# A drain of GpSimd's queue in front of its waits for gather buffers and indices, in a two-layer graph network

## The chip, the cores and the metric

The kernel runs on one NeuronCore of one Trainium2 chip. The metric is the device time of one execution in microseconds. A profile is one more execution, recorded by the hardware profiler; its durations are those of that execution alone.

## The reference, cut to what matters

There are 8 batches of 2048 nodes with 256 features, and a 0/1 adjacency matrix for each batch. Layer 0 takes, for each node, its first 25 neighbours and the elementwise maximum of their normalised rows. Layer 1 is an attention layer over the same adjacency matrix.

```python
h = jnp.maximum(_layernorm(x, axis=-1), 0.0)          # layer 0
pri = -jnp.arange(N, dtype=jnp.float32)
vals, idx = jax.lax.top_k(jnp.where(adj != 0, pri, -jnp.inf), 25)
agg = where(vals > -inf, vmap(lambda x, i: x[i])(h, idx), -inf).max(axis=2)
agg = where(degree <= 25, maximum(agg, 0.0), agg)
x = x + relu(concatenate([h, agg], -1) @ W0 + b0)
h = jnp.maximum(_layernorm(x, axis=-1), 0.0)          # layer 1
g = h @ W1; s1, s2 = g @ a1, g @ a2
att = softmax(where(adj > 0, leaky_relu(s1[:, :, None] + s2[:, None, :], 0.4), -1e20), axis=1)
x = x + gelu(att @ g)
```

## The kernel before, in words

A tile is 128 nodes; a batch has 16 tiles and the kernel 128. Each engine has a program of its own, written out by hand, and the programs meet in semaphores only. A round is one batch: in round b the engines work at layer 0 of batch b and, with `old` and `new`, at layer 1 of batch b - 1. Round 0 has layer 0 alone, and a last round without layer 0 (`drain=True` in the code, which has nothing to do with the instruction of that name) finishes layer 1 of batch 7.

**Layer 0 of a tile.** ScalarE turns a tile's adjacency rows into 0/1 (`sign`, L384), TensorE transposes them into PSUM `ps_c` (`transpose_signs`, L875), ScalarE copies them out (`evacuate_signs`, L388 and L390), TensorE packs them into words (`make_words`, L883 to L887), and VectorE searches the words for the first 25 neighbours (`search`, L596 to L647), which ends with the tile's list of indices `idx` and the semaphore `idx_ready`. `idx` has two buffers. GpSimd then gathers, for each of the 25 neighbours, 128 rows of 1 KB from the table of normalised rows `h_table` in HBM, one row for each partition: 25 indirect DMAs of 128 rows, all from L372. They fill two buffers: `gb0` takes the first 13 neighbours and `gb1` the other 12 (`CHUNKS = (13, 12)`). Each buffer exists once.

VectorE reduces a buffer by the maximum (`chunk_max`, L657). The reduction of `gb0` writes into a free slot of `gb1`, and the reduction of `gb1` writes `hl`. Each reduction ends with an increment of `maxed[0]` or `maxed[1]`, which tells GpSimd that the buffer is free. In VectorE's program, step v has the reduction of `gb1` of tile v first, then the search and the statistics, then the reduction of `gb0` of tile v + 1, and layer 1's work on both sides of it. A gather tells of its landing in the semaphores `gathered[0]` and `gathered[1]`, for which VectorE waits before a reduction.

**GpSimd's program** is nothing but these gathers. For each tile it waits for `idx_ready`, then for `maxed[0]`, issues 13 gathers, waits for `maxed[1]`, and issues 12. The helper `wait_apart` makes each wait an instruction of its own, followed by an increment of `pool_passed`, so that the wait stands in the sequencer and not in a gather. The sequencer may be some gathers ahead of the engine's processors, which write the descriptors. At the start of each batch there are two more waits, for the stores of `h_table` (`hn_stored`); the change leaves them alone.

**Layer 1 of a tile** takes two items (128 columns of attention each). For an item: ScalarE L437 turns edges into a bias, VectorE L717 (first half of a round, all 2048 columns) or L713 (second half, 1024 columns) adds it, ScalarE L444, VectorE L735, ScalarE L451 or L454 (exponential), VectorE L745, TensorE L895 into `ps_av`.

Of the kernel before, what the change touches and what calls it, by code (L numbers as in the profile page):

```python
# [68 lines left out]
def graph_layers(nc, x, adj, W0, b0, W1, a1, const_f, const_i, out):  # L69
    ctx = ExitStack()  # L70
    with ctx:
# [124 lines left out]
        def wait_apart(engine, name, semaphore, value):  # L196

            engine.wait_ge(semaphore, value)
            engine.sem_inc(S[name], 1)
# [155 lines left out]
        @block.gpsimd  # L355
        def _(pool):
            nc.gpsimd.memset(zeros[:, :], 0.0).then_inc(S["zeros_ready"], 1)
            pool.wait_ge(S["zrow_stored"], 32)
            with pool.Fori(0, NB, 2) as b2:
                for tb in range(2):  # L360
                    b = b2 + tb
                    for u in range(2):
                        wait_apart(pool, "pool_passed", hn_stored[u], b * 64 + 64)
                    with pool.Fori(0, PAIRS) as i:
                        for u in range(2):
                            g = b * TILES + i * 2 + u
                            wait_apart(pool, "pool_passed", S["idx_ready"], g + 1)
                            k = 0
                            for c, n in enumerate(CHUNKS):
                                wait_apart(pool, "pool_passed", maxed[c], g + 1)  # L370
                                for s in range(n):
                                    pool.indirect_dma_start(gb[c][:, s + (c > 0), :], None, table[tb],  # L372
                                                            bass.IndirectOffsetOnAxis(idx[u][:, k:k + 1], 0)
                                                            ).then_inc(gathered[c], 16)
                                    k += 1
# [635 lines left out]
```

## Time and profile before

| | |
|---|---|
| time, median of 3 runs | 4714.1 us (4710.35 to 4717.25) |
| span of the profiled execution | 5921.6 us |
| VectorE busy in it | 3609.4 us, 61% |
| GpSimd busy in it | 3420.3 us, 58% |
| TensorE busy in it | 2583.7 us, 44% |
| ScalarE busy in it | 2320.3 us, 39% |
| DMA queues, share of 16 engines | 23.8% (gathers), 18.1% (all other transfers) |
| gathers | 3200, 419.64 MB |

The profiled execution has no time of its own beside its span of 5921.6 us, from the first to the last instruction of the program; what lies around it isn't told. It is 1207.5 us longer than the median of the runs. Busy time counts instructions of the engines; the sequencers' waits and branches aren't counted.

### The profile page before, as it was taken

What the parts mean: (1) busy time and instruction counts of PE and PEld (TensorE: products, weight loads), DVE (VectorE), ACT (ScalarE), POOL (GpSimd) and SP (SyncE); (2) the same over time, 40 slices, a digit from 0 to 9 for tenths busy, and PEclk for the clock granted to TensorE, in tenths of its full rate; (3) what the DMA queues carried; (4) which work ended last, traced back from release to release, by engine and by line L of the source; (5) the groups of instructions that cost most, each with busy time, mean ns of one, the idle gap of its engine ahead of it and who ended that gap; (6) DMA issues with size and microseconds to landing.
All of it is one profiled execution on the core that took longest, in us unless ns stands there. A gap on an engine that the chain in (4) does not pass through costs nothing.

```text
span 5921.6 us, 48215 instructions
## 1 busy us (share of the span) xinstructions
PE 2583.7 (44%) x13568; PEld 1939.9 (33%) x13568; DVE 3609.4 (61%) x6299; ACT 2320.3 (39%) x2505; POOL 3420.3 (58%) x3205
## 2 busy tenths in 40 slices
PE   1332334444445334434455344444445435444357
PEld 1221223333333233323333233333334323333236
DVE  4454557566666566555677555666567656666567
ACT  2121234333444335333354333544335333434248
POOL 3655565555666566664677546466567665665530
PEclk9555556566666676666667666666666667666679
DMA  4434434344444444444444444344444444443322
GB/s 148 131 114 135 133 120 132 111 132 144 144 128 125 132 152 127 129 125 140 149 143 153 134 130 142 111 135 152 143 124 152 134 136 148 138 129 122 118 75 71
DMA packets 397876, 775.86 MB, mean 131 GB/s; under 512 B 64739, under 2 KB 245862, under 8 KB 381286
## 3 DMA queue, kind: packets, MB, share of 16 engines
q0 software_dynamic: 153600, 419.64, 23.8%
q1 hardware_dynamic: 244070, 353.77, 18.1%
q8 instruction: 93, 1.52, 0.1%
q14 instruction: 113, 0.93, 0.0%
HBM read 689.26 MB, written 83.89 MB: 131 GB/s over the span
## 4 chain that ended last, share of the span: by engine, by line
another core or an unknown queue 34%; issue 17%; ACT 14%; PE 12%; DVE 9%; POOL 1%; DMA 0%; ACTq 0%; DVEq 0%; SPq 0%; POOLq 0%
PE ps_av L895 4%; PE ps_l L923 3%; ACT stage L390 2%; ACT lk L444 2%; ACT lk L451 2%; ACT nbt L437 2%; PE ps_l L941 1%; ACT sg L384 1%; DVE hl L657 1%; DVE val L717 1%; PE ps_l L924 1%; POOL gb L372 1%; PE ps_l L943 1%; ACT y L498 1%
## 5 line engine op out<-in xcount | busy, mean ns | idle before, releaser
L372 POOL DMA_INDIRECT gb<-h_table,idx x3200 | 3419.6, 1069 | 2275.2 <-DVE gb L657 1039.9
L895 PE MATMUL ps_av<-hz,lk 128*128 128x256 f32 x3840 | 1136.2, 456 | 158.1 <-issue 85.7
L895 PEld LDWEIGHTS ps_av<-hz,lk 128*128 128x128 f32 x3840 | 878.6, 235 | 403.5 <-issue 252.5
L934 PE MATMUL ps_t<-cf,y 128*128 128x128 f32 x256 | 84.3, 430 | 2055.4 <-ACT y L498 1615.6
L388 ACT ACTIVATE sg<-ps_c 128x2048 bf16<-128x2048 bf16 x128 | 240.2, 1877 | 1813.7 <-remote 1673.1
L735 DVE SCALAR_TENSOR_TENSOR lk<-val,lk 128x2048 f32<-128x2048 f32 (+1 forms) x240 | 421.2, 1755 | 674.9 <-ACT lk L444 613.2
L657 DVE TENSOR_REDUCE hl<-gb 128x256 f32<-128x3328 f32 x128 | 746.8, 5834 | 83.6 <-DMA gb<-h_table,idx 67.2
L657 DVE TENSOR_REDUCE gb<-gb 128x256 f32<-128x3328 f32 x128 | 741.0, 5789 | 30.9 <-DMA gb<-h_table,idx 26.0
L934 PEld LDWEIGHTS ps_t<-cf,y 128*128 128x128 f32 x256 | 36.0, 197 | 2080.2 <-ACT y L498 1634.1
L923 PE MATMUL ps_l<-w,hcat 128*128 128x256 f32 x1024 | 407.2, 567 | 600.6 <-ACT hcat L485 505.2
L923 PEld LDWEIGHTS ps_l<-w,hcat 128*128 128x128 f32 x1024 | 277.5, 284 | 693.1 <-ACT hcat L485 483.4
L444 ACT ACTIVATE lk<-val,s2p 128x2048 f32<-128x2048 f32 (+1 forms) x240 | 379.4, 1581 | 271.5 <-remote 165.7
L717 DVE CUSTOM_DVE_ANT_0 val<-nbt,s_all 128x2048 f32<-128x2048 bf16 x120 | 274.0, 2283 | 292.0 <-ACT nbt L437 158.1
L437 ACT ACTIVATE nbt<-edge 128x2048 bf16<-128x2048 uint8 (+1 forms) x240 | 356.7, 1486 | 59.4 <-DVE m_t L717 39.8
L522 ACT COPY h_acc<-ps_l 128x257 f32<-128x257 f32 (+1 forms) x128 | 47.8, 373 | 825.2 <-remote 554.2
L941 PE MATMUL ps_l<-w,h1t 128*128 128x257 f32 x512 | 270.1, 666 | 71.7 <-issue 55.1
L804 DVE SCALAR_TENSOR_TENSOR x<-ps_l,xl 128x256 f32<-128x256 f32 x128 | 54.1, 422 | 325.4 <-PE ps_l L924 213.2
L384 ACT ACTIVATE sg<-ad 128x2048 bf16<-128x2048 int32 x128 | 243.3, 1901 | 6.1 <-DMA ad<-in_adj 6.1
L451 ACT ACTIVATE lk<-lk,nb 128x2048 f32<-128x2048 f32 x120 | 240.2, 2001 | 13.1 <-DVE lk L735 13.1
L390 ACT ACTIVATE stage<-ps_c 128x2048 uint8<-128x2048 bf16 (+1 forms) x128 | 239.6, 1872 | 0.0
L918 PE MATMUL ps_t<-cf,hl 128*128 128x128 f32 x512 | 102.3, 324 | 275.6 <-DVE hl L657 197.4
L713 DVE TENSOR_TENSOR val<-nbt,s_all 128x1024 f32<-128x1024 bf16 x120 | 146.0, 1216 | 108.5 <-ACT nbt L437 91.3
(95 smaller groups left out, 3767.9 us busy)
## 6 DMA issues: line engine op xcount, KB each, us to landing
ad<-in_adj SPq DMA_DIRECT2D x128, 1024.0 KB
edge<-edges_t SPq DMA_DIRECT2D x128, 512.0 KB
gb<-h_table,idx POOLq DMA_INDIRECT x3200
edges_t<-stage SPq DMA_DIRECT2D x32, 1024.0 KB
xl<-in_x SPq DMA_DIRECT2D x128, 128.0 KB
hl<-h_table SPq DMA_DIRECT2D x128, 128.0 KB
x_rows<-x SPq DMA_DIRECT2D x128, 128.0 KB
xo<-x_rows SPq DMA_DIRECT2D x16, 1024.0 KB
```

Of the source, the lines that this page charges most:

```text
L372: pool.indirect_dma_start(gb[c][:, s + (c > 0), :], None, table[tb], bass.IndirectOffsetOnAxis(idx[u][:, k:k + 1], 0)).then_inc(gathered[c ...
L384: nc.scalar.activation(sg[:, :], ad[u][:, :], ACT.Sign).then_inc(S["signed"], 1)
L390: nc.scalar.activation(stage[:, :, bass.ds(col, P)], sgt.rearrange("p (m n) -> p m n", n=P), ACT.Relu).then_inc(S["edges_ready"], 1)
L437: nc.scalar.activation(blocked_of(jj, drain)[:, cols], edge[u][:, jj, cols], ACT.Identity, scale=BLOCKED, bias=-BLOCKED).then_inc(S["block ...
L444: nc.scalar.activation(lk_of(jj, u, drain)[:, 0:w], val[jj][:, 0:w], ACT.Relu, scale=1 - SLOPE, bias=s2p[:, bass.ds(j, 1)]).then_inc(S["re ...
L451: nc.scalar.activation(q[:, :], q[:, :], ACT.Exp, bias=bias, accum_out=za[:, bass.ds(j, 1)]).then_inc(S["exp_ready"], 1)
L657: V.tensor_reduce(dst, gb[c][:, :, :].rearrange("p k c -> p c k"), AX.X, ALU.max).then_inc(maxed[c], 1)
L717: V.tensor_tensor_reduce(out=val[jj][:, :], in0=off[:, :], in1=s1_all[:, :], scale=1.0, scalar=-3e38, op0=ALU.add, op1=ALU.max, accum_out= ...
L735: V.scalar_tensor_tensor(out=q[:, 0:w], in0=val[jj][:, 0:w], scalar=SLOPE, in1=q[:, 0:w], op0=ALU.mult, op1=ALU.add).then_inc(S["leaky_rea ...
L895: ins = T.matmul(ps_av[:, k * C:(k + 1) * C], lk_of(jj, u, drain)[:, k * P:(k + 1) * P], hz[jj][:, :], start=False, stop=False)
L923: T.matmul(ps_l[:, 0:C], hcat[:, k, :], w0[:, k, :], start=k == 0, stop=False)
L941: T.matmul(ps_l[:, 0:C + 1], h1t[:, k, :], w1[:, k, :], start=k == 0, stop=k == 1)
```

## The change

GpSimd's sequencer gets a drain instruction in front of the wait for `maxed[0]` and in front of the wait for `maxed[1]`: two in each tile, 256 in all. A drain holds the sequencer until what it has handed to the engine is done. The wait for the indices moves behind the first of the two. All waits, their values, the gathers and their order stay as they are.

```diff
                         for u in range(2):
                             g = b * TILES + i * 2 + u
-                            wait_apart(pool, "pool_passed", S["idx_ready"], g + 1)
                             k = 0
                             for c, n in enumerate(CHUNKS):
+                                pool.drain()
+                                if c == 0:
+                                    wait_apart(pool, "pool_passed", S["idx_ready"], g + 1)
                                 wait_apart(pool, "pool_passed", maxed[c], g + 1)
                                 for s in range(n):
                                     pool.indirect_dma_start(gb[c][:, s + (c > 0), :], None, table[tb],
```

## Rows read from the trace of the kernel before

**Rows 1.** The page: span, busy time by engine, chain that ended last.

```profile
span 5921.6 us, 48215 instructions
...
PE 2583.7 (44%) x13568; PEld 1939.9 (33%) x13568; DVE 3609.4 (61%) x6299; ACT 2320.3 (39%) x2505; POOL 3420.3 (58%) x3205
...
another core or an unknown queue 34%; issue 17%; ACT 14%; PE 12%; DVE 9%; POOL 1%; DMA 0%; ACTq 0%; DVEq 0%; SPq 0%; POOLq 0%
```

**Rows 2.** Waits of ScalarE: waited for, us in total, times, longest.

```profile
ACT sg L388 <- remote: 1673.1, 98, 40.8
...
ACT sg L388 <- PE ps_c L875: 84.7, 25, 5.2
```

**Rows 3.** Timeline of one tile, TensorE, ScalarE, VectorE, GpSimd: start, length, instruction.

```profile
2880.30 1.06 PE L875 MATMUL ps_c<-cb,sg 128*128 128x128 bf16 x16
...
2903.96 1.88 ACT L388 ACTIVATE sg<-ps_c 128x2048 bf16<-128x2048 bf16 x1 [25.33 <-remote]
...
2896.49 0.95 POOL L372 DMA_INDIRECT gb<-h_table,idx  x1 [0.30 <-issue]
2900.61 1.16 POOL L372 DMA_INDIRECT gb<-h_table,idx  x1 [3.17 <-issue]
...
2891.19 0.15 DVE L584 TENSOR_SCALAR lt<-lt 128x1 f32<-128x1 f32 x1 [1.24 <-DVE lt L581]
```

**Rows 4.** GpSimd's gathers: length in ns (least, median, most), first and last start.

```profile
L372 POOL DMA_INDIRECT gb<-h_table,idx x3200: 940/946/3067, 53.6 to 5695.2; - x189
```

**Rows 5.** Costliest groups: busy, mean ns, idle time before and what ended it.

```profile
L372 POOL DMA_INDIRECT gb<-h_table,idx x3200 | 3419.6, 1069 | 2275.2 <-DVE gb L657 1039.9 <-issue 1002.2 <-DVE hl L657 229.2
```

**Rows 6.** Waits of GpSimd: waited for, us in total, times, longest.

```profile
POOL gb L372 <- DVE gb L657: 1039.9, 91, 31.4
POOL gb L372 <- issue: 1002.2, 3033, 52.3
POOL gb L372 <- DVE hl L657: 229.2, 63, 24.1
```

**Rows 7.** GpSimd from 5093 to 5204 us: 75 gathers, idle time before them.

```profile
L372 POOL DMA_INDIRECT gb<-h_table,idx x75: 942/946/2837, 5093.3 to 5202.9; - x75
...
  issue: 21.9, 72
  DVE gb L657: 3.0, 2
  DVE hl L657: 0.3, 1
```

**Rows 8.** Stretches: busy us of each engine, after the last gather.

```profile
core 0: us, PE busy (x) PEld busy (x) DVE busy (x) ACT busy (x) POOL busy (x), PEclk, DMA share, GB/s
...
5697.00:5921.60 224.60, 169.66 (x672) 135.01 (x672) 159.02 (x189) 175.81 (x149) 0.00 (x0) 0.87 0.19 63
```

**Rows 9.** Timeline of VectorE in the same stretches as rows 7 and 10.

```profile
2601.93 5.73 DVE L657 TENSOR_REDUCE hl<-gb 128x256 f32<-128x3328 f32 x1 [11.44 <-DMA gb<-h_table,idx]
...
5119.58 5.74 DVE L657 TENSOR_REDUCE gb<-gb 128x256 f32<-128x3328 f32 x1 [2.79 <-DMA gb<-h_table,idx]
```

**Rows 10.** Timeline: a gather beside VectorE's work on two tiles in SBUF.

```profile
2583.87 0.94 POOL L372 DMA_INDIRECT gb<-h_table,idx  x1 [0.30 <-issue]
2585.11 3.06 POOL L372 DMA_INDIRECT gb<-h_table,idx  x1 [0.30 <-issue]
...
2585.08 2.27 DVE L717 CUSTOM_DVE_ANT_0 val<-nbt,s_all 128x2048 f32<-128x2048 bf16 x1
```

**Rows 11.** GpSimd from one buffer to the other, where the wait had already ended.

```profile
2839.23 0.95 POOL L372 DMA_INDIRECT gb<-h_table,idx  x1 [0.30 <-issue]
2840.48 0.94 POOL L372 DMA_INDIRECT gb<-h_table,idx  x1 [0.30 <-issue]
```

**Rows 12.** GpSimd restarting after a wait, and the reduction that ended it.

```profile
2854.23 0.95 POOL L372 DMA_INDIRECT gb<-h_table,idx  x1 [0.30 <-issue]
2865.24 1.17 POOL L372 DMA_INDIRECT gb<-h_table,idx  x1 [10.06 <-DVE gb L657]
...
2858.60 5.85 DVE L657 TENSOR_REDUCE gb<-gb 128x256 f32<-128x3328 f32 x1
```

**Rows 13.** GpSimd: the last of the 13 gathers before the reduction at 5119.58.

```profile
5114.26 0.94 POOL L372 DMA_INDIRECT gb<-h_table,idx  x1 [0.30 <-issue]
```

**Rows 14.** The waits of GpSimd's sequencer: how many, length in ns.

```profile
L199 POOLq EVENT_SEMAPHORE  x400: 17/17/17, 49.7 to 5671.9; - x134
```

## Prediction

> **What bounds the kernel now.** I read the page first. No engine is over 61% busy, and the chain that ended last spends 34% of the span on "another core or an unknown queue", which this kernel on one core hasn't got [rows 1]. So the profiled execution spends a third of itself in waits that its records can't explain. The waits of ScalarE say where: L388, the copy of the transposed signs, waits 1673.1 us in 98 tiles, and only 84.7 us in 25 more is put down to TensorE [rows 2]. The timeline of one tile shows what such a wait is. TensorE has transposed the signs at 2880.30 + 1.06 = 2881.36 us, and the copy that waits for nothing else starts at 2903.96, 22.6 us later, after GpSimd's run of gathers has ended at 2897.44 and the next has begun. In the same tile VectorE, which waits for its own previous result of 0.15 us, gets it 1.24 us later, about the pace of one gather [rows 3]. Semaphores arrive late while GpSimd works.
>
> The second fact is that this execution lasts 5921.6 us and the runs without a recorder 4714.1, 1207.5 us less. So much of that lateness can't be there in the runs that are timed. I take it as the recorder's own doing, and this is argued, not shown. The Trainium skill, NOTIFIC — the notification-queue block, section 7.1, says that the block which takes the engines' records holds its producers back rather than lose what is in its internal pipeline; no row here shows that block.
>
> What bounds the timed run, then? I add up what GpSimd must do even if nobody holds it up. The first gather starts at 53.6 us [rows 4]. The 3200 gathers are busy for 3419.6 us, a mean of 1.069 although the median is 0.946 [rows 4, 5]: some take 2 to 3 us, such as the one of 3.06 us beside VectorE's addition of 2.27 us [rows 10]. Between two gathers that follow each other there are 21.9 / 72 = 0.304 us [rows 7]; 3199 of these are 972.5 us. After the last gather come 5921.6 - (5695.2 + 0.9) = 225.5 us of layer 1 [rows 4, 8]. The sum is 53.6 + 3419.6 + 972.5 + 225.5 = 4671.2 us. That is 42.9 us under the median of 4714.1, under 1%. So GpSimd's stream with almost no wait in it gives the time of the timed run. Per tile it is (3419.6 + 972.5) / 128 = 34.3 us, against 3609.4 / 128 = 28.2 us of VectorE [rows 1]. Where the semaphores happen not to be late, the profile shows the same order. In 75 gathers, three tiles from 5093.3 to 5202.9 + 1.0 = 5203.9 us, GpSimd is never kept for more than the restart of a moment (3.0 us in 2 waits, [rows 7]), a tile takes 36.9 us, and VectorE waits for gathers, once for 11.44 us [rows 9]. In the profile as a whole it is the other way round: GpSimd waits 1039.9 + 229.2 us for reductions [rows 6], because VectorE, behind its late semaphores, is late with them.
>
> **The change, part by part.** It adds 256 drains and moves the 128 waits for the indices behind half of them. It removes no wait and no work, and it moves no transfer past another queue: SP's queue doesn't know of it. Behind each drain stand, on GpSimd, one or two waits and the 12 or 13 gathers of a buffer; for those gathers wait VectorE's reduction and, through it, the tile.
>
> Now the cost of one. Today, where the wait has already ended, the sequencer has passed it while the processors were still at earlier gathers, and the first gather of the next buffer follows after the usual gap: 0.30 us, from 2839.23 + 0.95 = 2840.18 to 2840.48 [rows 11]. With a drain the sequencer stands still until the last gather is done, and only then reads the wait and hands over a gather. What that takes is shown by a restart. The reduction ends at 2858.60 + 5.85 = 2864.45, and the first gather starts at 2865.24: 0.79 us, with the sequencer ready at its wait and the processors empty [rows 12]. The first gather there takes 1.17 instead of 0.95 us; I don't charge this, since VectorE's next addition runs at that moment as in [rows 10], and where the wait had ended earlier it doesn't. The wait itself takes 0.017 us [rows 14].
>
> The drain isn't in the trace. From below I bound its own cost at 0: it ends as the last gather's record ends. From above, it would count a gather as done only when its rows have landed. The last of 13 gathers ends at 5114.26 + 0.94 = 5115.20 and the reduction that waits for it starts at 5119.58, so landing takes up to 4.38 us [rows 9, 13]. I take 0.2 us for the drain's end and for the second wait of a tile and the register work, near the lower end, because what is drained is the queue of instructions, and a gather's instruction has its record's end at 0.95 us. So one drain costs 0.79 + 0.2 - 0.30 = 0.69 us. With nothing for the drain and the waits it costs 0.49, and with the landing 0.49 + 4.38 = 4.87 us.
>
> The Trainium skill, PSUM — Partial Sum Buffer, section Engine vs sequencer instructions, says that a drain waits for the engine to go fully idle. It names no time, and the trace before has no drain of GpSimd to set beside it; by it a cost of none at all is excluded.
>
> How much of it is on the path? The first drain meets an empty queue. The other 255 lie in a stream that sets the end: 255 x 0.69 = 176 us. Cover could come from waits that are there anyway, since a drain in front of a wait which would have been long costs nothing. The timed run has room for 42.9 us of them by the sum above. If they all cover drains, the cost is 133 us. I take the middle, since some of the 42.9 us will be something else: about 155 us. The move of the wait for the indices is part of this: they are found a tile ahead, and VectorE has time to spare. What is late next is the landing of each buffer, 0.7 us more each time, and VectorE waits longer for gathers; its 28.2 us a tile and its waits have room in 34.3 + 1.4 us. The tail of 225.5 us has no gather and stays. So 4714 + 155 = 4869 us; against the sum of the profile, 4671.2 + 176 = 4847 us. I predict 4870.
>
> **The rivals.**
>
> *Waits cover the drains: no change.* In the profile 91 + 63 = 154 of 256 boundaries end in a wait for a reduction [rows 6], and there a drain is free. At the other 102 it delays gathers by 0.69 us, 70 us in all, most of which the next wait swallows. If the timed run were like this, with VectorE's chain as the bound, it would stay between 4714 and 4730 us. Against it: that chain's lateness is what the timed run seems to lack, and GpSimd's own sum leaves 42.9 us for waits, not 1269. It decides if the gathers without a recorder take less: at 0.05 us less each, 160 us of waits would be free for cover.
>
> *The drain quiets the semaphores: faster.* The unexplained waits fall in GpSimd's runs of gathers [rows 3]. If they are partly real in the timed run, and come from a long queue or from a sequencer that waits on a semaphore while the processors write descriptors, then shorter runs with an idle moment in between release them sooner. The place is L388 and VectorE's short instructions after the search. The price: GpSimd's floor with every gather at its median is 53.6 + 3200 x (0.946 + 0.304) + 225.5 = 4279 us; with the drains it is 4279 + 176 = 4455. Half of the way from 4714 to there is 4585 us. It decides when the timed run holds over 155 us of such waits and the drains take them all. Against it: the sum leaves 42.9 us of waits, if the gathers are as long there as here.
>
> *The drain waits for the landing: much slower.* 255 x 4.87 = 1242 us gives 5956; with half of the landing counted, 255 x 2.68 = 683 us and 5397. For it speaks only that nothing in the trace excludes it.
>
> *The drain doesn't hold the sequencer for gathers that its processors are at.* Then it is a short instruction that runs ahead with the others, and the time stays at 4714 us.
>
> **How the numbers follow.** The forecast, GpSimd's stream longer by 0.3 to 1.3 us a drain, has 0.76: its own range is 4780 to 5020. Cover has 0.09, the drain that doesn't hold 0.03, quieter semaphores 0.08, landing counted 0.04. Of cover, I give half to within 0.2% and half to a little more. About 0.2%, 9 us, is what can be told from no change here. That makes slower 0.76 + 0.04 + 0.045, together 0.84, within 0.2% 0.08, and faster 0.08. The range for all takes in cover and the drain that doesn't hold, and goes up to a drain of 1.3 us: 4705 to 5040. It leaves out 0.08 below and some 0.06 above.
>
> **What the next profile would show.** Right, if no gather that is the first of a buffer starts less than about 0.8 us after the one before it ends (0.30 now), with a gap near 1.0 us where the semaphore had come; if the 3200 gathers keep their mean near 1.07 us; and if GpSimd's sum, made as above with these gaps, gives the new time. Wrong in size, if that gap is 0.8 or 2 us. Wrong in mechanism, if the gap is as said and the time doesn't follow (then something else bounds the timed run), or if L388 starts at once after TensorE's transposes while GpSimd gathers, and the time falls (then late semaphores were real). The span of the profile is no judge: it has the recorder's waits in it, and may fall where the time rises.

## The result

The changed kernel takes 5568.6 us, the median of 4 runs (5562.4 to 5570.0), against 4714.6 before: a ratio of 1.1816, 95% interval 1.1802 to 1.183. That is 854 us more. The forecast was 4870 us, in a range of 4705 to 5040. The direction was right and the size wrong by more than a factor of five.

The page of the changed kernel: span, busy time, the chain that ended last, and the group of the gathers (their line is L374 now).

```profile
span 5568.2 us, 48535 instructions
...
PE 2754.3 (49%) x13568; PEld 2070.3 (37%) x13568; DVE 3580.5 (64%) x6299; ACT 2345.9 (42%) x2505; POOL 3441.1 (62%) x3205
...
POOL 53%; issue 33%; POOLq 10%; PE 2%; ACT 1%; DVE 1%; DMA 0%; SPq 0%; DVEq 0%; ACTq 0%
...
L374 POOL DMA_INDIRECT gb<-h_table,idx x3200 | 3440.4, 1075 | 1918.8 <-issue 1918.8
```

The chain is GpSimd from end to end: 53% gathers, 33% "issue" and 10% its sequencer, against 34% "another core or an unknown queue" in [rows 1]. No wait of GpSimd is for VectorE any more; in [rows 6] 1269 us were. All its idle time, 1918.8 us, is "issue", the word for idle time that the profile puts down to nothing; a drain's wait falls under it. The span is 5568.2 us, as long as the timed runs. In [rows 1] it was 1207 us longer than they were.

What happens at a drain stands in the timeline, GpSimd and VectorE's reductions alone. First the boundary from gb0 to gb1, then the one from gb1 to gb0 of the next tile:

```profile
2817.25 1.00 POOL L374 DMA_INDIRECT gb<-h_table,idx  x1 [0.30 <-issue]
...
2821.45 5.91 DVE L659 TENSOR_REDUCE gb<-gb 128x256 f32<-128x3328 f32 x1 [2.97 <-DMA gb<-h_table,idx]
2822.79 0.94 POOL L374 DMA_INDIRECT gb<-h_table,idx  x1 [4.54 <-issue]
...
2839.17 0.95 POOL L374 DMA_INDIRECT gb<-h_table,idx  x1 [0.30 <-issue]
...
2842.09 5.72 DVE L659 TENSOR_REDUCE hl<-gb 128x256 f32<-128x3328 f32 x1 [9.05 <-DMA gb<-h_table,idx]
2843.47 0.94 POOL L374 DMA_INDIRECT gb<-h_table,idx  x1 [3.36 <-issue]
```

The last gather of gb0 ends at 2818.25. VectorE's reduction waits for the landing and starts at 2821.45, 3.20 us later. The next gather starts 1.34 us after that. At the other boundary the landing takes 1.97 us, and the next gather starts 1.38 us after the reduction. So GpSimd doesn't move when its queue is empty. In these two places it moves 1.3 to 1.4 us after the reduction that waits for the landing has started.

The drains' own records, name, count and length in ns (least, median, most), and below them the one of the first boundary above:

```profile
L369 POOLq DRAIN  x256: 41/14724/19374, 52.6 to 5330.7; - x128
```

```profile
L369 POOLq DRAIN  x1: 17621/17621/17621, 2804.4 to 2804.4; - x1
```

The second ends at 2804.4 + 17.6 = 2822.0 us, 0.6 us after the reduction's start and 0.8 us before the next gather. It is so at every boundary. The trace has the time at which each gather's landing is counted in its semaphore. Between the last gather's record and its landing lie 1.7 to 5.9 us, 2.35 in the mean. From that landing to the drain's end it is 0.57 us at all 128 boundaries from gb0 to gb1 and 0.53 at all 127 others, the same to 0.01 us, however long the landing took. From the drain's end to the next gather it is 0.80 and 1.00 us. That the drain holds until the landing is thus seen 255 times.

A drain with nothing to wait for takes 41 ns. The median of 14.7 us is mostly gathers that had to be done in any case. The cost is what GpSimd's idle time shows: 1918.8 us, less 52.5 before the first gather, less 2944 gaps inside the buffers of 0.304, leaves 971.3 us for 255 boundaries. That is 3.81 us for each, where the usual gap is 0.30.

### The profile page after: what moved, and what is told of

Its sections match the earlier page's. It is cut to its first block, busy times and chain, and to the rows that moved or that the text cites. A ratio compares the mean times of both kernels' runs of the same rounds, so it can differ in the third digit from the quotient of the medians.

```text
span 5568.2 us, 48535 instructions
## 1 busy us (share of the span) xinstructions
PE 2754.3 (49%) x13568; PEld 2070.3 (37%) x13568; DVE 3580.5 (64%) x6299; ACT 2345.9 (42%) x2505; POOL 3441.1 (62%) x3205
## 4 chain that ended last, share of the span: by engine, by line
POOL 53%; issue 33%; POOLq 10%; PE 2%; ACT 1%; DVE 1%; DMA 0%; SPq 0%; DVEq 0%; ACTq 0%
POOL gb L374 53%; POOLq L369 10%; PE ps_av L897 1%; POOLq L198 0%; ACT nbt L439 0%; ACT lk L446 0%; ACT gb L453 0%; ACT gb L439 0%; DVE val L719 0%; POOLq L199 0%; POOLq L364 0%; ACT gb L446 0%; DMA ad<-in_adj 0%; ACT lk L453 0%; DVE hl L659 0%
## 5 line engine op out<-in xcount | busy, mean ns | idle before, releaser
L374 POOL DMA_INDIRECT gb<-h_table,idx x3200 | 3440.4, 1075 | 1918.8 <-issue 1918.8
L659 DVE TENSOR_REDUCE hl<-gb 128x256 f32<-128x3328 f32 x128 | 732.8, 5725 | 1310.3 <-DMA gb<-h_table,idx 1310.3
L897 PE MATMUL ps_av<-hz,lk 128*128 128x256 f32 x3840 | 1200.0, 481 | 355.8 <-DVE hz L747 355.3
L897 PEld LDWEIGHTS ps_av<-hz,lk 128*128 128x128 f32 x3840 | 935.3, 250 | 620.7 <-issue 438.1
L920 PE MATMUL ps_t<-cf,hl 128*128 128x128 f32 x512 | 141.7, 432 | 1672.3 <-DVE hl L659 1672.3
L487 ACT COPY hcat<-ps_t 128x512 f32<-128x512 f32 x128 | 74.9, 585 | 1563.5 <-PE ps_t L920 1563.5
L920 PEld LDWEIGHTS ps_t<-cf,hl 128*128 128x128 f32 x512 | 91.5, 217 | 1721.7 <-DVE hl L659 1210.2
L925 PE MATMUL ps_l<-w,hcat 128*128 128x256 f32 x1024 | 477.6, 646 | 86.9 <-ACT hcat L487 86.9
L925 PEld LDWEIGHTS ps_l<-w,hcat 128*128 128x128 f32 x1024 | 321.1, 329 | 208.5 <-ACT hcat L487 130.2
L936 PE MATMUL ps_t<-cf,y 128*128 128x128 f32 x256 | 72.4, 376 | 576.9 <-ACT y L500 576.9
```

The costliest lines, as they stand in the source:

```text
L659: V.tensor_reduce(dst, gb[c][:, :, :].rearrange("p k c -> p c k"), AX.X, ALU.max).then_inc(maxed[c], 1)
L897: ins = T.matmul(ps_av[:, k * C:(k + 1) * C], lk_of(jj, u, drain)[:, k * P:(k + 1) * P], hz[jj][:, :], start=False, stop=False)
L925: T.matmul(ps_l[:, 0:C], hcat[:, k, :], w0[:, k, :], start=k == 0, stop=False)
```

## The experiments

There were ten runs, in three groups. Two theories stood at first. Theory 1: GpSimd's stream sets the end of the timed run, and a drain lasts until the gathers have landed. The rival: the loss is a time of the drain's own, or comes by way of VectorE.

**One of the two drains alone.**

```diff
-                                pool.drain()
+                                if c == 0:        # drain_gb0_only; c == 1 in drain_gb1_only
+                                    pool.drain()
```

> The drain stands only in front of the wait for gb0 (and for the indices), once a tile. Theory 1, GpSimd's stream sets the end of the timed run and a drain holds it until the last gather has landed: in the changed kernel this gap is 3.78 us in the mean instead of 0.304, so 127 x 3.48 = 441 us, 5156 us, and the gap from gb0 to gb1 is 0.30 again. Rival, the loss comes from losing the run-ahead in front of both buffers together, or from VectorE's chain being late twice a tile: less than half of the 854 us, below 5050. The recorder's excess (span far over the timed run) says nothing for either; I expect some of it to be back.

> The drain stands only in front of the wait for gb1. Theory 1: the gap from gb0 to gb1 is 3.83 us in the changed kernel, so 128 x 3.53 = 451 us, 5165 us; the two halves together then give the 854 us of the whole within some 40 us. Rival, one half is covered by a wait that is there anyway (the wait for gb0 was the long one in the profile before): this half under 4900 us and the other near 5500, or the reverse.

Measured: 5230.2 us (ratio 1.111, 1.1085 to 1.1136) and 5319.2 us (1.1292, 1.1262 to 1.1322). Neither half is covered by a wait, as theory 1 says, and the rivals' numbers, below 5050 and below 4900, are both missed. But they are 74 and 154 us above its numbers, and together cost 1121 us, where 854 within 40 was expected. Each drain costs more when it is alone: GpSimd's idle time gives (1571.1 - 53.5 - 3072 x 0.304) / 127 = 4.60 us for a boundary at gb0 (3.78 in the changed kernel), and at gb1 it is 5.22 us (3.83). With 25 gathers behind it, the drain ends 1.06 us after the landing in both kernels, about 0.5 us later than with 12 or 13. The rest is the landing itself: 2.51 us in the mean after the last gather's record instead of 2.25 at gb0, and 3.36 instead of 2.46 at gb1. Why it takes longer there was not tried. Theory 1 is right in kind and lacks a term.

**The same wait without a drain.** This is the kernel before, with one wait more; the wait for the indices stands where it stood.

```diff
                                     k += 1
+                                pool.wait_ge(gathered[c], (g + 1) * (16 * n))
```

> No drain. After the last gather of each buffer GpSimd's sequencer waits on the semaphore that counts the landings of that buffer's gathers, all of them. Theory 1, the drain is a wait for the landing and some 0.6 us of its own: the next gather starts about 0.8 us after the last landing (1.37 and 1.51 us with the drain), so some 0.6 us less at each of 255 boundaries: 5568 - 153 = 5415 us, range 5380 to 5460. Rival, the drain's cost has little to do with the landing and is a time of its own of some 3 us: this kernel need not come near 5415, and with a landing of 2.4 us after the record and 0.8 us for the restart it would agree only by chance.

Measured: 5532.4 us (1.1754, 1.1725 to 1.1783), 117 us over the number and outside its range. A wait for the landings by a semaphore costs nearly what the drains cost: 818 us against 854. Its restart is as quick as was thought, 0.78 us after the reduction here:

```profile
2546.34 0.95 POOL L372 DMA_INDIRECT gb<-h_table,idx  x1 [0.30 <-issue]
...
2549.18 5.87 DVE L658 TENSOR_REDUCE gb<-gb 128x256 f32<-128x3328 f32 x1
...
2549.96 0.94 POOL L372 DMA_INDIRECT gb<-h_table,idx  x1 [2.67 <-DMA gb<-h_table,idx]
```

At 31 of the 128 boundaries from gb0 to gb1, those of every fourth tile, the restart took 3.24 us from the landing instead of 0.80, as here, from a reduction at 2507.98 to a gather at 2511.20:

```profile
2507.98 5.86 DVE L658 TENSOR_REDUCE gb<-gb 128x256 f32<-128x3328 f32 x1
...
2511.20 0.94 POOL L372 DMA_INDIRECT gb<-h_table,idx  x1 [5.06 <-issue]
```

That is 31 x 2.44 = 76 of the 117 us. At the other boundaries, to gb0, it took 0.95 us in every second tile and 1.27 to 1.81 in those between, 1.145 in the mean: another 127 x (1.145 - 0.80) = 44 us over the 0.8 that was expected. Together they are the miss. Why these start late isn't settled.

**Two drains in a row.**

```diff
                                 pool.drain()
+                                pool.drain()
```

> Two drains one behind the other at each of the 256 places. Theory 1, the first waits for the landing and the second finds nothing open: at most 0.1 us each, 5570 to 5600 us. Rival, each drain has a fixed cost of 2 to 3.5 us whatever is open: 5568 + 256 x 2 = 6080 us or more.

Measured: 5580.2 us (1.1852, 1.1826 to 1.1877), 11.6 us above the changed kernel for 256 more drains. The rival's fixed cost is refuted. The second drain's records:

```profile
L370 POOLq DRAIN  x256: 34/41/41, 52.6 to 5352.4; - x128
```

**Is GpSimd's stream the bound before the change?**

```diff
-CHUNKS = (13, 12)
+CHUNKS = (12, 12)
```

> The kernel before with 12 + 12 gathers instead of 13 + 12; it leaves the 25th neighbour out, and the reduction of gb0 is one slot shorter. It asks whether GpSimd's stream set the end before the change. Theory 1, it does: 128 x (1.07 + 0.304) = 176 us less, 4538 us, range 4510 to 4570. Rival, VectorE's chain sets it: its reduction gets shorter by 5.8 / 13 = 0.45 us a tile, 57 us at most, so 4657 us or more.

Measured: 4585.7 us (0.9722, 0.9699 to 0.9744), 129 us less, 48 us above theory 1's number and outside its range. The rival allowed 57 us at most. The gathers are busy for 3366.6 us at 1.096 us each, while a gather that meets nothing takes 0.949. What a gather takes on top lies beside VectorE's work (see the last section) and doesn't shrink with the gathers: 3366.6 - 3072 x 0.949 = 451 us here, 430 in the kernel before. So a gather that is left out is worth a bare one, 128 x (0.949 + 0.304) = 160 us at most, and not the mean. GpSimd's idle time before gathers that the view puts down to VectorE and the indices is 78 us in this kernel, mostly 0.3 us at a time, the usual gap; what goes beyond is 17 us.

**Narrow rows, without and with drains.**

```diff
-pool.indirect_dma_start(gb[c][:, s + (c > 0), :], None, table[tb],
+pool.indirect_dma_start(gb[c][:, s + (c > 0), 0:32], None, little,   # little: (ROWS, 32)
```

> The kernel before, where each gathered row is 128 bytes from a table of its own instead of 1 KB from h_table (the rest of gb stays at zero, so layer 0's neighbours aren't the reference's). The number of descriptors is the same, an eighth of the bytes moves. Theory 1: a gather occupies GpSimd as long as before, 1.07 us and 0.304 between two, so the time stays within 40 us of 4714; what changes is the landing. Rival, the transfer of the rows bounds the stream: clearly faster, below 4600 us.

> The same narrow gathers with the 256 drains. Theory 1, the drain lasts until the last gather has landed: with a landing some 1 us shorter (1.3 instead of 2.35 us after the record's end) each of the 255 gaps is 1 us shorter, so about 255 x (1.3 + 1.44 - 0.30) = 622 us above the narrow kernel without drains, some 5330 us, and the next gather starts 1.37 and 1.51 us after the last landing as before. Rival, the cost is the drain's own: 854 us above the narrow kernel without drains.

Measured: 4682.3 us (0.9926, 0.9904 to 0.9949) and 5391.6 us (1.1425, 1.1401 to 1.1449). An eighth of the bytes takes 32 us off the kernel without drains, so the transfer doesn't bound the stream. With drains it takes 177 us off. The cost of the drains falls from 854 to 709 us, since the landing is shorter: (1740.5 - 53.1 - 2944 x 0.304) / 255 = 3.11 us a boundary instead of 3.81. It fell by 0.7 us where 1 us was expected. All of the fall is in the landing, 1.65 us in the mean instead of 2.35; the drain still ends 0.53 and 0.57 us after it. A cost that is the drain's own wouldn't have moved.

**How many gathers lie behind a drain.** After the two halves theory 2 came up: once the gathers have landed, a drain still goes through all those since the last drain, one by one. The rival: it levels off.

```diff
-                                pool.drain()
+                                if c == 0 and u == 0:
+                                    pool.drain()
```

> One drain in two tiles, in front of gb0 of the first tile of a pair: 64 drains, 50 gathers between two. After the last landing the next gather started 1.37 us later where 13 gathers lay behind the last drain and 1.86 where 25 did, at gb1; at gb0 1.51 with 12 and 2.05 with 25. So theory 2 says that a drain goes through the gathers since the last drain once all have landed, 0.041 us each: with 50 it is 0.95 + 0.04 + 50 x 0.041 = 3.0 us. Rival, it levels off at about 2.05 us because only the gathers that are still open count. Time by theory 2: 4714 + 63 x (2.5 + 3.0 - 0.3) = 5042 us; by the rival 4714 + 63 x 4.25 = 4982 us. If a kernel with long unbroken runs has late semaphores under the recorder, the span of its profile should be over the timed runs here too.

Measured: 5042.0 us (1.0694, 1.0673 to 1.0716), theory 2's number; the rival's was 4982. That it is met to the microsecond is in part luck: the landing took 2.2 us, not 2.5, and the step after it 3.3 us, not 3.0. Then one drain a batch, in the kernel before:

```diff
                     for u in range(2):
                         wait_apart(pool, "pool_passed", hn_stored[u], b * 64 + 64)
+                    pool.drain()
```

> One drain for each batch, behind the two waits for h_table: 8 drains, 400 gathers between two. Theory 2, a drain goes through all gathers since the last one, 0.042 us each, after the last has landed: 400 x 0.042 = 17 us, plus 2.3 for the landing and 0.9 for the restart, less 0.3: 20 us at each of 7 boundaries, 4714 + 140 = 4854 us. Rival, it goes through a bounded number of them (50 and more looked at so far): at 64 it would be 2.7 us, 7 x 5.6 = 39 us, 4753 us.

Measured: 4779.3 us (1.0148, 1.0129 to 1.0166), 65 us for 7 drains that count. Neither number is met: 4854 by theory 2, 4753 by the rival. The timelines of three kernels show the step from the landing (VectorE's reduction of gb1 waits for it) to the next gather. One drain a tile, 25 gathers behind it:

```profile
2544.30 5.72 DVE L660 TENSOR_REDUCE hl<-gb 128x256 f32<-128x3328 f32 x1 [7.80 <-DMA gb<-h_table,idx]
2546.14 0.94 POOL L375 DMA_INDIRECT gb<-h_table,idx  x1 [3.82 <-issue]
```

One drain a pair, 50 gathers:

```profile
2562.26 5.78 DVE L660 TENSOR_REDUCE hl<-gb 128x256 f32<-128x3328 f32 x1 [2.80 <-DMA gb<-h_table,idx]
2565.45 0.94 POOL L375 DMA_INDIRECT gb<-h_table,idx  x1 [5.18 <-issue]
```

One drain a batch, 400 gathers:

```profile
2847.42 5.79 DVE L658 TENSOR_REDUCE hl<-gb 128x256 f32<-128x3328 f32 x1 [2.71 <-DMA gb<-h_table,idx]
...
2854.87 1.68 POOL L373 DMA_INDIRECT gb<-h_table,idx  x1 [9.34 <-issue]
```

These steps are 1.84, 3.19 and 7.45 us. How much of them is the drain's shows in its record, in the mean over all boundaries of a kernel:

| gathers since the last drain | boundaries | from the landing to the drain's end |
|---|---|---|
| 12 (changed kernel, at gb0) | 127 | 0.53 us |
| 13 (changed kernel, at gb1) | 128 | 0.57 us |
| 25 (one drain a tile, at gb0) | 127 | 1.06 us |
| 50 | 63 | 2.29 us |
| 400 | 7 | 6.42 us |

Behind it comes the restart, 0.80 us to gb1 and 0.96 to 1.12 us to gb0, nearly as after a plain wait (0.80 and 0.95 at the least). The drain's own part grows with 0.04 to 0.05 us a gather up to 50 and with (6.42 - 2.29) / 350 = 0.012 us after that, so theory 2 holds only for the first part. Where it bends, and why, was not tried, and neither was what the drain does in that time.

The move of the wait for the indices was not run by itself. The plain wait for the landings and the one drain a batch leave that wait where it stood, and show the cost without the move.

**The kernel before, with a second profile.**

> The kernel before, unchanged, with a profile of its own. The profiles of the eight kernels so far have spans within 0.5% of their timed runs, and none has ScalarE waits at L388 for a remote release; only the first profile of the kernel before was 1207 us over. Theory 1: that profile was the exception, and a new one has a span near 4714 us, with GpSimd's gaps near 0.31 us throughout, first gather 54 us, gathers 3440 us, gaps 980 us, tail 208 us, which sum to 4682. Rival: this kernel always loses some 1200 us under the recorder, and the span is near 5900 again.

Measured: 4711.3 us (0.9996, 0.9985 to 1.0006). The span of its profile is 4711.4 us, theory 1's expectation:

```profile
span 4711.4 us, 48215 instructions
```

Its waits of GpSimd (idle us, count, longest):

```profile
POOL gb L372 <- issue: 973.2, 3014, 52.9
POOL gb L372 <- DVE idx L646: 25.6, 84, 0.3
POOL gb L372 <- DVE hl L657: 23.2, 76, 0.3
POOL gb L372 <- DVE gb L657: 13.8, 26, 2.0
```

Who waited for its gathers:

```profile
  DVE hl L657: 579.4, 114
  DVE gb L657: 88.6, 50
```

And ScalarE's wait at L388:

```profile
ACT sg L388 <- PE ps_c L875: 382.0, 116, 7.3
```

VectorE waits 668 us for gathers. GpSimd waits for reductions 37.0 us here, where [rows 6] had 1269. ScalarE's L388 waits for TensorE and for nothing remote, where [rows 2] had 1673.1 us. So the first profile of this kernel was of an unusual execution: none of the eleven profiles since has a span far from its timed runs or a wait for something remote.

## Why the prediction was wrong

**The stream of GpSimd as the bound: right.** The prediction worked this out of a profile that was 1207 us too long, and came to 4671 us. The second profile has 54.2 us to the first gather, 3466.4 of gathers, 982.9 between them and 208.0 behind. That these sum to the span is no evidence, since they would in any trace. The evidence is the 982.9: it is 10 us more than 3199 usual gaps, 972.5, so the stream hardly waits. That the prediction's sum came out 42.9 us short was not room for waits: the gathers took 47 us more than in the first profile and the gaps 10 more, and the tail 17 less. The changed kernel has 53.8, 3440.4, 1866.3 and 207.7: 883 us more in the gaps, 26 less in the gathers. That the drains lie on the path, each with its full cost, was right as well. By the boundaries' mean 255 x (3.81 - 0.304) = 894 us went in; some 10 of them were idle time there before, and with the 26 off that leaves about 858. The timed runs say 854.

**The step that failed is the cost of a drain.** The prediction had 0.79 for the restart, 0.2 for the drain and the waits, less 0.30: 0.69 us. The restart is about right: 0.80 us to gb1 and 1.00 to gb0, where two waits stand behind the drain. What is wrong is "near the lower end, because what is drained is the queue of instructions". The drain ends after the landing, and 0.53 to 0.57 us after it. Measured are 3.51 us a drain, five times 0.69: 2.35 for the landing, 0.55 for the drain's own part and 0.90 for the restart, less 0.30. The prediction had the mechanism as its third rival, "the drain waits for the landing", with a chance of 0.04 and 5397 to 5956 us; the measured 5569 lies inside. It priced the landing at 4.38 us, from one reduction, at 5119.58, and had nothing for what comes between the landing and the drain's end. The two go opposite ways: the mean landing is 2.35 us, and the drain's part 0.55. What the drain waits for takes in the DMAs that GpSimd has issued: narrow rows, with the same instructions, shorten it. The Trainium skill, PSUM — Partial Sum Buffer, section Engine vs sequencer instructions, has a drain wait for the engine to go fully idle; the traces agree, if the landings count as part of that.

**The weight was wrong more than the working.** No row told 0 from 4.38 us, and the value was chosen near one end by an argument on what a queue is. Where both ends are possible and a drain stands on the path 255 times, they make 125 and 1242 us. The range should have held both.

**"Semaphores arrive late while GpSimd works": true of that one execution, not of the kernel.** The prediction took the excess as the recorder's doing and called that argued. As something that the recorder always does it is refuted: the recorder was on in all the profiles since, and their spans are the timed runs'. "The span of the profile is no judge" falls with it; the changed kernel's span was a good one. The prediction also read one row in the wrong place: VectorE's wait of 11.44 us for gathers stands at 2601.93 us, not in the stretch from 5093 to 5204, where its two waits for gathers are 2.79 and 4.18 us. What disturbed that execution stays open. The rival that built on it, quieter semaphores, falls with it.

**Cover by waits: absent.** GpSimd waited 62.6 us for VectorE and its indices before the change (25.6 + 23.2 + 13.8), nearly all of it 0.3 us at a time, which is the usual gap between two gathers and no wait at all. After it, no wait for either shows. So not even the 20 us that the prediction took off were there.

## What to carry to other kernels

A drain of GpSimd's queue behind indirect DMAs was here a wait for their landing, and then some. Put none into a stream that sets the end without such a price in the sum, and where one is needed, put few: per drain it costs more with more gathers behind it, but 7 cost 65 us here and 255 cost 854. A plain wait for the landing was hardly cheaper, 818 us, so what costs is stopping the stream until the rows are there. When a profile's span is far from the timed runs, take a second one before reading its waits; what survived in the first, within 1%, was the sum of the bounding engine's own work. And when the cost of a new instruction is bounded only from far apart, multiply both ends by the count before choosing.

## What the runs showed that was not expected

After the landing a drain on GpSimd lasts 0.53 us with 12 gathers since the last drain, 1.06 with 25, 2.29 with 50 and 6.42 with 400, and 0.041 us with none. With 12, 13 or 25 it is the same at every boundary to 0.01 us, and rows of 128 bytes don't change it.

A gather of 128 rows occupies GpSimd for the same 0.94 to 0.95 us whether its rows have 1 KB or 128 bytes; the narrow kernel's median is 944 ns. The first line counts 1 KB, the second 128 bytes:

```profile
L372 POOL DMA_INDIRECT gb<-h_table,idx x3200: 942/949/3079, 54.2 to 4502.5; - x189
```

```profile
L374 POOL DMA_INDIRECT gb<-little,idx x3200: 940/944/3077, 54.8 to 4471.4; - x189
```

The mean of 1.083 us against the median of 0.949 makes 430 us in 3200 gathers (3466.4 - 3200 x 0.949). The long ones lie beside VectorE's operations on two tiles in SBUF, as in [rows 10]: in the second profile 414 of the 430 us lie in the 486 gathers that overlap most with L717, L713, L735 or L752, while the 631 beside the reduction of gb1, which reads one tile, take 951 ns in the mean. The Trainium skill, SBUF — State Buffer, section SBUF: two separate sides, describes a lock between VectorE and GpSimd, held by VectorE's instructions in a 2-port mode, and by those with two inputs in SBUF only against a GpSimd instruction that reads SBUF. The trace agrees in that gathers are long beside instructions with two inputs, 2.3 us in the mean beside L717; which access of a gather waits no row shows, and no run took that work away. It may be where this kernel's time could still fall.
